# Source histogram, lane counts and running base of a graph network kernel: one product with 128 columns of weights in place of two with 64

## The chip, the core and the metric

The kernel runs on one core of one Trainium2 chip. The metric is the device time of one execution in microseconds (us); the figure compared is the median of several runs. TensorE's rows in the profile show two granted clocks, 0.50 (1.2 GHz) and 1.00 (2.4 GHz), and means between them where a stretch holds both.

## What is computed

Four graph layers on 12500 nodes with 64 features, 400000 edges sorted by destination, each layer with a normalisation ahead of it and a residual behind it:

```python
h = jnp.maximum(_layernorm(x), 0.0)
x = x + L0(h)   # edge network relu([x_i, x_j - x_i] @ W1 + b1) @ W2 + b2, then segment_max over dst
h = jnp.maximum(_layernorm(x), 0.0)
x = x + L1(h)   # sum over edges of x[src] * rsqrt(out_deg[src]), times rsqrt(in_deg), @ W + b, leaky relu
h = jnp.maximum(_layernorm(x), 0.0)
x = x + L2(h)   # two rounds of mean over incoming edges, each with a dense layer
h = jnp.maximum(_layernorm(x), 0.0)
x = x + L3(h)   # x @ W_self.T + b_self + segment_sum(x[src] * edge_weight, dst) @ W_neigh.T + b_neigh
```

`out_deg` is the number of edges that leave each node: a histogram of `src`. It is one of the things that the changed products compute.

## The kernel before

128 partitions ("lanes") hold 3125 consecutive edges each, and the edge loops walk them in 125 blocks of 25 columns (`K`), five blocks (`R`) to an iteration of a hardware loop. Each engine's program is written by hand; semaphores alone order them.

**Stage of layer 0 (`body0`).** For each block, GpSimd (POOL) gathers 25 columns of rows of `tab_edge_b` into a ring of five slots with one indirect DMA each (L632) and one more for the keys (L640). VectorE (DVE, `slot0`) adds, scans maxima column by column (L1393) and, between those, makes one-hot batches with one instruction each (`row_onehots`, L685): first the batches of the block's own `src` numbers (`hist_batch`: 16 columns, then 9; one-hots of the quotient, 128 wide, and of the remainder, 98 wide), then eight batches of 16 columns for `block_counts` (`count_batch`). TensorE (PE) runs in this order: two transposes of keys (L1939, L1940), the first batch of transposes of the ring (`turn`, L1929), `hist_counts(b, 0)` over 16 columns and `hist_counts(b, 1)` over 9, then in turn more transposes, the edge products (L1952) and `block_counts`. ScalarE (ACT) empties what PE makes: transposes at L1753, counts at L1737, 4 banks for each batch of 16 columns.

For each column c, `hist_counts` adds into PSUM `mixed` the product of the quotient's one-hots (weights) with the remainder's (moving, 98 columns), which is the histogram, and the product of an identity `ident_b` with the same remainder's one-hots, which counts by lane. Both go through a helper that makes each as two products with 64 columns of weights, the output's partitions 0 to 63 and 64 to 127:

```python
def halves(to, by_q, by_r, start, stop):
    for k in range(0, P, D):
        last = e.matmul(to[k:k + D, :], by_q[:, k:k + D], by_r, start=start, stop=stop, skip_group_check=True)
    return last
```

That is 4 products for a column, 100 for a block. The last product of each of the two calls raises `histed`; DVE's `count_batch(b, r, 0)` waits for the first (it overwrites the one-hots that the first 16 columns used) and `count_batch(b, r, 1)` for the second. `block_counts` uses `halves` as well, 256 products for a block, into the two banks `bk`.

**Stage of layer 3 (`body4`).** For each block DVE computes target rows for 25 columns of messages, and POOL scatters them with 25 indirect DMAs (L1180). PE's only work in the loop is the running base: when DVE has raised `looked`, 25 pairs of halves add `ident_b` times the block's one-hots `oh_lane` to PSUM `kp`, and the last raises `based`; DVE waits for it before it makes the next block's one-hots.

Between the two stages stand the dense sums of layers 1 to 3 (L769, L775, L728, L730), which the change does not touch. Ahead of `body0`, `count_tensor` (L479) makes products with 128 columns of weights and 98 moving columns, in groups of five; behind `body4`, `unit` (L2004) makes products with 128 columns of weights and 64 moving columns.

Of the kernel before, what the change touches and what calls it, by code (L numbers as in the profile page):

```python
# [19 lines left out]
K = 25  # L20
# [17 lines left out]
HIST = [range(0, VS), range(VS, K)]  # L38
# [19 lines left out]
def build(nc, x, src, dst, edge_weight, l0_w1, l0_b1, l0_w2, l0_b2, l1_w, l1_b,  # L58
# [7 lines left out]
    with ctx:  # L66
# [60 lines left out]
        ident_b = sb("ident_b", [P, P], bf16)  # L127
# [73 lines left out]
        hist, pa, pb = mixed[:, 0:TILES], mixed[:, TILES:TILES + P], mixed[:, TILES + P:TILES + 2 * P]  # L201
        cnt = mixed[:, TILES + 2 * P:2 * TILES + 2 * P]
        kp = ps("kp", [P, 512])
        base, iota_p = kp[:, 0:TILES], kp[:, P:2 * P]
# [10 lines left out]
        def mm_banks(name, u):  # L215
# [20 lines left out]
        ohq = [h_half[:, u * P * VS:(u + 1) * P * VS].rearrange("p (k q) -> p k q", q=P) for u in range(2)]  # L236
        ohr = [h_half[:, 2 * P * VS + u * TILES * VS:2 * P * VS + (u + 1) * TILES * VS]
               .rearrange("p (k q) -> p k q", q=TILES) for u in range(2)]
# [22 lines left out]
        oh_lane = m_half[:, 2 * K * TILES:3 * K * TILES].rearrange("p (k q) -> p k q", q=TILES)  # L261
# [39 lines left out]
        def gate(e):  # L301

            e.sem_inc(sem("gate_" + e.engine.name), 1)
# [1563 lines left out]
        def _(e):  # L1867
# [27 lines left out]
            def halves(to, by_q, by_r, start, stop):  # L1895

                for k in range(0, P, D):
                    last = e.matmul(to[k:k + D, :], by_q[:, k:k + D], by_r, start=start, stop=stop, skip_group_check=True)  # L1898
                return last

            def hist_counts(b, h):

                wait(e, "batched", b * (VB + 2) + (h + 1))
                gate(e)
                for c in range(len(HIST[h])):
                    first = isinstance(b, int) and b + h + c == 0
                    halves(hist, ohq[h][:, c, :], ohr[h][:, c, :], first, c == len(HIST[h]) - 1)
                    last = halves(cnt, ident_b, ohr[h][:, c, :], False, c == len(HIST[h]) - 1)
                last.then_inc(sem("histed"), 1)

            def block_counts(b, v):
# [75 lines left out]
            def body4(i):  # L1987
                for r in range(R):
                    wait(e, "looked", i * R + (r + 1))
                    gate(e)  # L1990
                    for j in range(K):
                        last = halves(base, ident_b, oh_lane[:, j, :], False, j == K - 1)
                    last.then_inc(sem("based"), 1)
            loop(e, body4)

# [36 lines left out]
```

## Time and profile before

| | |
|---|---|
| device time, median of 3 runs | 18454.92 us (18447.9 to 18476.08) |
| profiled execution: span from first to last instruction | 13809.8 us |
| what lies around the span (median less span) | 4645.1 us |
| PE busy, weight loads busy | 7082.0 us, 5084.7 us |
| DVE busy | 9045.7 us (66%) |
| ACT busy | 5948.2 us (43%) |
| POOL busy | 7815.4 us (57%) |
| stage `body0` | about 560 to 5280 us of the span |
| stage `body4` | about 9010 to 13100 us |

The profile gives the span of the profiled execution and no device time of its own for it, so its own time is taken as the median, with the 4645.1 us around the span. In the rows below a group of instructions is "engine line operation out<-in, weights, moving columns, type, xcount"; PE is a product, PEld a load of its weights, and "idle before <-releaser" is the time in which the engine stood still before it and what ended that. "issue" is idle time that no event in the profile explains.

### The profile page before, as it was taken

How to read it: one execution, taken by the hardware profiler on the slowest of the kernel's cores; microseconds unless marked ns; L12 is line 12 of the kernel's file. 1: busy time of each engine (PE TensorE's matmuls, PEld its weight loads, DVE VectorE, ACT ScalarE, POOL GpSimd, SP SyncE). 2: the span in 40 equal slices, each digit the busy share in tenths (PEclk: the TensorE clock that was granted, in tenths of full speed). 3: DMA queues.
4: the chain of work that ended last, by engine and by line, in shares of the span. 5: the costliest groups of instructions: out<-in, count | busy, mean ns of one | idle time of the engine just before them, and what ended most of it. 6: DMA issues, size and time to landing. Idle time of an engine off the chain costs nothing. (4 is left out here: it accounts for less than half of the span.)

```text
span 13809.8 us, 283975 instructions
## 1 busy us (share of the span) xinstructions
PE 7082.0 (51%) x96792; PEld 5084.7 (37%) x96792; DVE 9045.7 (66%) x17848; ACT 5948.2 (43%) x10705; POOL 7815.4 (57%) x7194
## 2 busy tenths in 40 slices
PE   2266666666666663998899999700000000000066
PEld 1155555555555552554455555400000000000055
DVE  5388888888888886444444344466666666666585
ACT  0144444444444443776777677522222222222201
POOL 5677777777777773111111111367777777777700
PEclk9866666666666666999899899755555555555598
DMA  7333333333333333886688588422222222222197
GB/s 308 144 112 113 112 114 114 119 112 112 113 112 115 115 114 94 261 265 220 200 263 267 172 265 263 160 72 66 63 66 66 66 63 66 63 63 66 60 361 241
DMA packets 1274431, 1981.83 MB, mean 144 GB/s; under 512 B 256937, under 2 KB 987918, under 8 KB 1268737
## 3 DMA queue, kind: packets, MB, share of 16 engines
q1 hardware_dynamic: 867553, 1059.78, 24.4%
q10 hardware_dynamic: 174288, 612.09, 12.0%
q0 software_dynamic: 231664, 297.80, 8.1%
q8 instruction: 558, 9.14, 0.3%
q14 instruction: 368, 3.01, 0.1%
HBM read 1167.21 MB, written 815.55 MB: 144 GB/s over the span
## 5 line engine op out<-in xcount | busy, mean ns | idle before, releaser
L632 POOL DMA_INDIRECT RF<-tab_edge_b,idx x3125 | 3541.2, 1133 | 1030.6 <-issue 948.6
L1180 POOL DMA_INDIRECT records<-RF,idx x3125 | 3130.6, 1002 | 984.5 <-issue 984.5
L1737 ACT ACTIVATE X<-bk 128x392 uint8<-128x392 f32 x4000 | 1782.6, 495 | 1565.0 <-PE bk L1898 1548.0
L685 DVE TENSOR_TENSOR HM<-iota_b,eqw 128x2048 bf16<-128x2048 bf16 x2000 | 2201.7, 1101 | 342.7 <-PE bk L1898 197.6
L1898 PE MATMUL bk<-HM 128*64 128x98 bf16 x32000 | 1583.2, 247 | 1306.7 <-ACT X L1737 672.8
L1898 PE MATMUL kp<-HM,ident_b 128*64 128x98 bf16 x6250 | 281.7, 283 | 3805.4 <-DVEq L1646 3805.4
L876 POOL DMA_INDIRECT agg<-RF,lastT x372 | 536.9, 1443 | 2856.9 <-ACT RF L808 2766.0
L769 PE MATMUL tp<-HM,RF 128*64 128x512 bf16 x12276 | 2001.2, 379 | 7.9 <-ACT HM L728 2.0
L1898 PEld LDWEIGHTS bk<-HM 128*64 128x64 bf16 x32000 | 1239.8, 134 | 1653.2 <-issue 1571.3
L1898 PEld LDWEIGHTS kp<-HM,ident_b 128*64 128x64 bf16 x6250 | 261.7, 168 | 3826.3 <-issue 3826.3
L775 PE MATMUL om<-HM,RF 128*64 128x512 bf16 x6138 | 1442.3, 379 | 0.0
L769 PE MATMUL tp<-RF 128*64 128x512 bf16 x5952 | 1032.7, 381 | 201.4 <-ACT RF L728 201.4
L769 PEld LDWEIGHTS tp<-HM,RF 128*64 128x64 bf16 x12276 | 854.2, 110 | 651.6 <-issue 52.3
L730 DVE CAST HM<-dst_f 128x4096 bf16<-128x4096 uint8 x186 | 426.8, 2294 | 739.1 <-DMA dst_f<-counts 390.1
L1828 ACT ACTIVATE RF<-qblk 128x50 f32<-128x50 f32 x125 | 31.7, 254 | 1978.9 <-DMA records<-RF,idx 1904.2
L1393 DVE SCALAR_TENSOR_TENSOR RF<-RF,dupjunk 128x64 f32<-128x64 f32 x3124 | 865.8, 277 | 27.3
L1393 DVE SCALAR_TENSOR_TENSOR RF<-RF,dupjunk,om 128x64 f32<-128x64 f32 x3124 | 841.2, 269 | 0.4
L728 ACT ACTIVATE RF<-dst_f 128x4096 bf16<-128x4096 uint8 x186 | 672.7, 3617 | 343.1 <-PE tp L769 342.0
L728 ACT ACTIVATE HM<-dst_f 128x4096 bf16<-128x4096 uint8 (+1 forms) x186 | 702.2, 3822 | 102.5 <-PE tp L769 102.5
L775 PE MATMUL om<-RF 128*64 128x512 bf16 x2976 | 722.6, 381 | 0.0
L728 ACT ACTIVATE HM<-crow 128x4096 bf16<-128x4096 uint8 x186 | 670.6, 3606 | 6.4 <-DMA crow<-counts 4.5
L1898 PE MATMUL mixed<-HM 128*64 128x98 bf16 x6250 | 498.6, 272 | 329.8 <-DVE HM L685 278.2
(362 smaller groups left out, 14805.4 us busy)
## 6 DMA issues: line engine op xcount, KB each, us to landing
dst_f<-counts SPq DMA_DIRECT2D x465, 512.0 KB, 4.6
RF<-first_rows SPq DMA_DIRECT2D x250, 800.0 KB
counts<-X ACTq DMA_DIRECT2D x250, 784.0 KB
records<-RF ACTq DMA_DIRECT2D x88, 1960.0 KB, 8.2
RF<-records SPq DMA_DIRECT2D x220, 784.0 KB
crow<-counts SPq DMA_DIRECT2D x279, 512.0 KB, 4.7
first_rows<-RF ACTq DMA_DIRECT2D x25, 4000.0 KB, 49.5
edge_rows<-RF ACTq DMA_DIRECT2D x125, 800.0 KB, 8.0
```

What stands on the lines that cost most here:

```text
L632: e.indirect_dma_start(out=ring[:, r, j, :], out_offset=None, in_=table[:, :], in_offset=bass.IndirectOffsetOnAxis(ap=idx[:, r, j:j + 1], ...
L685: return e.tensor_tensor(to[:, 0:n, :].rearrange("p k (q h) -> p k q h", h=2), iota_b[:, 0:m].rearrange("p (q h) -> p q h", h=2).unsqueeze ...
L728: e.activation(to, of, ACT.Copy).then_inc(sem("widened_A"), 1)
L730: e.tensor_copy(to, of).then_inc(sem("widened_D"), 1)
L769: last = e.matmul(tp[u][k * D:(k + 1) * D, :], hi_mid[:, t, k * D:(k + 1) * D], part, start=t == 0, stop=t == TILES - 1, skip_group_check= ...
L775: return e.matmul(om[u][k * D:(k + 1) * D, :], low[:, t, :], part, start=t < 2, stop=t >= TILES - 2, skip_group_check=True)
L876: e.indirect_dma_start(out=agg[:, :], out_offset=bass.IndirectOffsetOnAxis(ap=lastT[:, g * GB + k:g * GB + k + 1], axis=0), in_=out_rows[g ...
L1180: e.indirect_dma_start(out=records[:, :], out_offset=bass.IndirectOffsetOnAxis(ap=idx2[:, r, j:j + 1], axis=0), in_=msgs[MSG_OF[r]][:, j, ...
L1393: e.scalar_tensor_tensor(out=buf[:, r, j, :], in0=prev, scalar=mask[:, j:j + 1], in1=this, op0=op0, op1=op1).then_inc(sem(chain.name), 1)
L1737: e.activation(staged[u].rearrange("p (r k) -> p r k", k=P)[:, :, k:k + 4], bk[s % 2][:, 0:4 * TILES].rearrange("p (k r) -> p r k", k=4), ...
L1828: e.activation(msgs[MSG_OF[r]][:, :, RW - 2:RW], qblk[:, r, :].unsqueeze(2).broadcast_to([P, K, 2]), ACT.Copy)
L1898: last = e.matmul(to[k:k + D, :], by_q[:, k:k + D], by_r, start=start, stop=stop, skip_group_check=True)
```

## The change

`hist_counts` and the running base of `body4` use a new helper that makes one product with all 128 columns of weights where there were two of 64. `block_counts` keeps `halves`.

```diff
+            def whole(to, by_q, by_r, start, stop):
+
+                return e.matmul(to, by_q, by_r, start=start, stop=stop, skip_group_check=True)
+
             def hist_counts(b, h):
...
                 for c in range(len(HIST[h])):
                     first = isinstance(b, int) and b + h + c == 0
-                    halves(hist, ohq[h][:, c, :], ohr[h][:, c, :], first, c == len(HIST[h]) - 1)
-                    last = halves(cnt, ident_b, ohr[h][:, c, :], False, c == len(HIST[h]) - 1)
+                    whole(hist, ohq[h][:, c, :], ohr[h][:, c, :], first, c == len(HIST[h]) - 1)
+                    last = whole(cnt, ident_b[:, :], ohr[h][:, c, :], False, c == len(HIST[h]) - 1)
                 last.then_inc(sem("histed"), 1)
...
                     for j in range(K):
-                        last = halves(base, ident_b, oh_lane[:, j, :], False, j == K - 1)
+                        last = whole(base, ident_b[:, :], oh_lane[:, j, :], False, j == K - 1)
                     last.then_inc(sem("based"), 1)
```

On PE, at the start of a block's `hist_counts` (`mixed` is the PSUM tile, `HM` holds the one-hots), the program before has, with the output's rows and columns behind the names:

```order
L1929 MATMUL tp<-ident,RF 128x128 x4
L1898 MATMUL mixed<-HM 64x98 x2
L1898 MATMUL mixed<-HM,ident_b 64x98 x2
L1898 MATMUL mixed<-HM 64x98 x2
L1898 MATMUL mixed<-HM,ident_b 64x98 x2
```

and the changed one, whose lines lie four further down and whose `whole` is L1903:

```order
L1933 MATMUL tp<-ident,RF 128x128 x4
L1903 MATMUL mixed<-HM 128x98
L1903 MATMUL mixed<-HM,ident_b 128x98
L1903 MATMUL mixed<-HM 128x98
L1903 MATMUL mixed<-HM,ident_b 128x98
```

Each x2 has become one product; the pattern goes on for 25 columns. Nothing else stands in another place on PE, and the programs of DVE, ACT and SP are the same.

## Rows read from the trace of the kernel before

**Rows 1.** The page: the span, and each engine's busy time and instructions.
```profile
span 13809.8 us, 283975 instructions
PE 7082.0 (51%) x96792; PEld 5084.7 (37%) x96792; DVE 9045.7 (66%) x17848; ACT 5948.2 (43%) x10705; POOL 7815.4 (57%) x7194
```
**Rows 2.** Busy time by window, one in each stage; then PEclk, DMA share, GB/s.
```profile
3000.00:3500.00 500.00, 310.43 (x5227) 261.84 (x5222) 435.05 (x1003) 220.10 (x489) 386.57 (x346) 0.68 0.36 112
10000.00:11000.00 1000.00, 67.60 (x1500) 62.81 (x1500) 638.12 (x1288) 288.43 (x1064) 766.88 (x766) 0.50 0.21 65
```
**Rows 3.** Waits from 1000 to 5000 us, in `body0`: us in total, times, longest.
```profile
POOL RF L632 <- issue: 806.6, 2647, 0.3
...
DVE lane_keys L1435 <- issue: 99.2, 21, 5.5
...
DVE HM L685 <- PE mixed L1898: 74.4, 94, 3.9
...
POOL RF L632 <- DMA cix<-chunk_lin: 34.9, 10, 5.5
POOL crow L640 <- issue: 32.3, 106, 0.3
```
**Rows 4.** List by line, whole span: busy us, mean ns, idle before, three releasers.
```profile
L632 POOL DMA_INDIRECT RF<-tab_edge_b,idx x3125 | 3541.2, 1133 | 1030.6 <-issue 948.6 <-DMA cix<-chunk_lin 52.7 <-DMA tab_edge_b<-HM 29.2
...
L685 DVE TENSOR_TENSOR HM<-iota_b,eqw 128x2048 bf16<-128x2048 bf16 x2000 | 2201.7, 1101 | 342.7 <-PE bk L1898 197.6 <-PE mixed L1898 101.5 <-PE om L1952 33.9
```
**Rows 5.** Timeline of PE in one block: start us, us; the 50 pairs of `hist_counts`.
```profile
3059.99 0.29 PE L1898 MATMUL mixed<-HM 128*64 128x98 bf16 x2 [2.22 <-DVE HM L685]
...
3060.21 0.32 PE L1898 MATMUL mixed<-HM,ident_b 128*64 128x98 bf16 x2
...
3063.96 0.27 PE L1898 MATMUL mixed<-HM,ident_b 128*64 128x98 bf16 x2
3064.16 0.66 PE L1929 MATMUL tp<-ident,RF 128*128 128x128 f32 x4
```
**Rows 6.** Timeline of DVE in the same block, at `count_batch(b, r, 0)`.
```profile
3062.96 1.22 DVE L685 TENSOR_TENSOR HM<-iota_b,eqw 128x2048 bf16<-128x2048 bf16 x1 [0.37 <-PE mixed L1898]
```
**Rows 7.** Timeline of PE, first block of an iteration: a pause inside `hist_counts`.
```profile
1138.28 0.32 PE L1898 MATMUL mixed<-HM,ident_b 128*64 128x98 bf16 x2
1140.50 0.29 PE L1898 MATMUL mixed<-HM 128*64 128x98 bf16 x2 [1.91 <-issue]
```
**Rows 8.** Timeline of DVE in that block.
```profile
1143.15 1.22 DVE L685 TENSOR_TENSOR HM<-iota_b,eqw 128x2048 bf16<-128x2048 bf16 x1 [2.49 <-PE mixed L1898]
```
**Rows 9.** Timeline of PE: products that have 128 columns of bf16 weights already.
```profile
42.19 0.59 PE L479 MATMUL mixed<-HM 128*128 128x98 bf16 x5 [0.99 <-DVE HM L465]
...
272.16 1.67 PE L1884 MATMUL mixed<-eqw,hT 128*128 128x128 bf16 x14 [2.19 <-DVE eqw L676]
...
13110.58 5.28 PE L2004 MATMUL bk<-RF 128*128 128x64 bf16 x96 [90.00 <-DVE RF L685]
```
**Rows 10.** Durations by line: ns min/median/max, first and last start; weights, moving columns.
```profile
L479 PE MATMUL mixed<-HM x125: 260/282/285, 40.6 to 79.0; 128*128 128x98 bf16 x125
...
L1898 PE MATMUL mixed<-HM x6250: 203/282/291, 569.4 to 5244.3; 128*64 128x98 bf16 x196
```
**Rows 11.** Busy time by window: around the last row of rows 9, and around rows 5.
```profile
13110.00:13116.00 6.00, 5.28 (x96) 5.18 (x97) 3.87 (x8) 0.70 (x3) 0.00 (x0) 0.50 0.99 319
...
3059.00:3064.00 5.00, 4.01 (x100) 4.04 (x100) 4.52 (x10) 1.09 (x2) 3.78 (x5) 0.50 1.01 407
```
**Rows 12.** Timeline of PE: one bank of `block_counts` at either granted clock.
```profile
3055.34 0.95 PE L1898 MATMUL bk<-HM 128*64 128x98 bf16 x16 [0.36 <-ACT X L1737]
...
3065.97 0.55 PE L1898 MATMUL bk<-HM 128*64 128x98 bf16 x16 [0.26 <-issue]
```
**Rows 13.** Timeline in `body4`: PE's running base, and DVE's next use of `kp`.
```profile
9107.92 2.25 PE L1898 MATMUL kp<-HM,ident_b 128*64 128x98 bf16 x50 [21.51 <-DVEq L1646]
...
9129.69 2.71 DVE L1645 TENSOR_TENSOR HM<-HM,kp 128x2450 f32<-128x2450 bf16 x1
```

## The prediction

> **What bounds the kernel now.** The two stages that the change touches have different limits, so I read the page's totals first and then each stage by itself. The page gives a span of 13809.8 us, with DVE and POOL the busiest engines in the sum [rows 1]. The window in `body0` shows PE busy 310 of 500 us, DVE 435, POOL 387; the window in `body4` shows PE busy 68 of 1000 us and POOL 767 [rows 2].
>
> In `body4` the 766 scatters of the window leave 1000 - 766.88 = 233 us, 0.304 us for each. That is the pause that POOL makes between any two of its indirect DMAs in `body0` as well ("issue", 806.6 / 2647 = 0.305 us) [rows 2, 3]. So POOL never waits for anybody there: it is the limit.
>
> In `body0` two engines run almost level. POOL has 386.57 us of work and 346 pauses of 0.305 us in 500 us, 492 in all. Its only waits for others are 34.9 us out of 4000, and 52.7 us in the whole span (the releaser DMA `cix<-chunk_lin`, index loads that SP sends when DVE has finished a scan) [rows 2 to 4]. DVE is the engine that these waits come from, and it never waits for the gathers. So DVE, with its own waits, sets the pace, and POOL stands right behind it. What DVE waits for is what the change can move: over the span its batches wait 197.6 us for `block_counts`, 101.5 us for `hist_counts` (`mixed`) and 33.9 us for the edge products (`om`) [rows 4]. The window from 1000 to 5000 us holds 106 blocks (one key gather each), 37.7 us for a block, and 94 of them have a wait for `mixed`, 74.4 us in all [rows 3].
>
> These waits are of two kinds. In an ordinary block DVE waits 0.37 us for the end of the first 32 pairs [rows 6]. In the first block of an iteration PE pauses after its eighth product with "issue" as the cause, here 1.91 us, and DVE then waits 2.49 us [rows 7, 8]. Such starts are the 21 in the window at which DVE itself stops for 99.2 us in total [rows 3]. With 0.37 us for 94 - 21 = 73 ordinary waits (27 us), 47 us are left for the 21 starts, 2.3 us each, which fits the row.
>
> **The pace of the products.** It carries everything else. Before, 50 pairs start between 3059.99 and 3063.96 us: 3.97 / 49 = 0.081 us for a pair, at a granted clock of 0.50, which is the lower level, 1.2 GHz [rows 5, 11]. 98 columns at 1.2 GHz take 98 / 1.2 = 82 ns, so a pair costs what one product costs: the two halves already run side by side, and halving the number of products saves no array time. What one whole product costs is shown by `count_tensor`, whose products have the very shape (128 columns of bf16 weights, 98 moving columns): five take 0.59 us, the last of them some 0.28, so (0.59 - 0.28) / 4 = 0.078 us for each [rows 9, 10]. Their median duration, 282 ns, is that of the halves as well [rows 10]. The bounds for the new step are 0.078 and, from the row with 128 moving columns, (1.67 - 0.31) / 13 = 0.105 us, where 0.31 is an estimate for the last product (282 ns and 30 more columns) [rows 9]. I take 0.081, nearest to the row with the same shape: cost 0.
>
> Could wide weights show behind a product? `unit` has 128 columns of bf16 weights and 64 moving ones: 96 products in 5.28 us, (5.28 - 0.24) / 95 = 0.053 us at granted clock 0.50 (0.24 is my estimate for the last one) [rows 9, 11]. So such a load fits into 0.053 us, well under the 0.081 of 98 columns. The Trainium skill, "TensorE: Matmul & The Clock Gate", section "LDWEIGHTS (loading the stationary operand)", says otherwise: a load costs its columns divided by 1.2 in ns, an estimate of 107 ns for 128, and by it the sum would be that of rival B. The same page's part on Fast Weight Load excepts loads of exactly 128 columns that aren't fp32, and the trace agrees with the exception. Whoever leaves these sentences out still has 0.053.
>
> **The change part by part, in `body0`.**
>
> 1. The last half. A pair's row lasts 0.32 us and a product 0.282 [rows 5, 10], so the second half starts 0.04 us behind the first, and the semaphore hangs on the second. A whole product ends with the first. In the ordinary blocks DVE's wait of 0.37 us ends 0.04 earlier: 73 x 125 / 106 = 86 blocks, 3 us.
> 2. The pause at an iteration's start. It comes after 8 products, which is after a fixed number of instructions [rows 7]. With whole products the 8 done before it are worth 16 halves, so 24 products remain of the first 32, where 28 pairs did: 4 x 0.081 = 0.32 us less of DVE's 2.3 us, at 24 starts: 8 us. The bounds are 0 (it sits elsewhere now) and its whole length, about 2 x 24 = 48 us.
> 3. From halves to transposes. The last pair starts at 3063.96 and the next transpose at 3064.16, 0.20 us against a step of 0.08 [rows 5]. If the surplus of 0.12 is the price of going from 64-column products to 128-column ones, it leaves this place. It makes the edge products earlier, for which DVE waits 33.9 us in all [rows 4]. Bounds 0 and 0.12 x 125 = 15 us; I take 6, since under half of the blocks have that wait at all. The Trainium skill, "TensorEngine Tiling (Array Packing)", section "Key Properties", says that changing the tiling mode drains TensorE; by it this term is wholly real, by the pause alone it may be something else.
> 4. `block_counts`, all DVE, ACT, POOL and SP instructions and every wait are as before: 0.
>
> **In `body4`** PE ends the base at 9107.92 + 2.25 = 9110.2 us and DVE reads `kp` at 9129.69 [rows 13]; 19 us cover a burst of 2.3. Were it half or double, nobody would notice. 0 us. If this cover went, the loop would still be POOL's.
>
> The sum is 3 + 8 + 6 = 17 us less. Late next is POOL: what DVE gains beyond POOL's 52.7 us of waits [rows 4] would be spent waiting for gathers. Against 18454.92 us (the span and 4645.1 us around it, taken as unchanged; I use the median because the profiled execution has no time of its own) that gives **18438 us**. Seventeen us are 0.1%; about 0.2%, 37 us, is what a measurement of this kernel can tell from no change.
>
> **The rivals.**
>
> - **A, the pause goes.** Half as many products and loads to bring in could let PE start an iteration without its pause, and the early blocks too. DVE would gain up to 48 us from term 2, and 9 from the others, 57, cut to POOL's 52.7: about 18402 us. For it speaks that the pause has "issue" as its cause; against it that DVE stops at the same place for 4.7 us each with a program that does not change [rows 3].
> - **B, wide weights show (slower).** Place: the first 32 products of each `hist_counts`, whose end DVE awaits. If a load of 128 columns cannot hide, a product costs 0.105 us, the upper bound above, against 0.081 for a pair: 0.024 x 32 = 0.77 us for a block, all of it on DVE, x 125 = 96 us, 18551 us. It decides from a step of about 0.091 on (0.3 us for a block, 37 us). For it speaks the width; against it both rows of 128-column weights at the lower clock.
> - **C, the clock (slower).** In this stage the clock is at its higher level part of the time, mean 0.68 [rows 2]. If PE with half as many instructions were granted it less often, one more bank group for each block would run as the 0.95 us row and not as the 0.55 us row [rows 12]. DVE's batches hide part of it; I take 0.3 us for a block, 37 us: 18492 us. Against it: the array streams the same columns for the same time.
> - **D, nothing at all**, or the change does not act as it reads (both halves still issued): 18455 us. The printed program speaks against the second.
>
> **How the numbers follow.** The forecast has 0.58, A 0.13, B 0.07, C 0.09, D 0.13. Forecast and D lie within 0.2%: 0.71, and half of C, just at the border, makes it 0.76. Faster by over 0.2% is A, 0.13. Slower is B and the rest of C, 0.11. The range reaches from A (18402, rounded to 18400) to C (18492, rounded to 18490); left out are B and what lies beyond A and C, under 2 in 10.
>
> **What the changed profile would show.** 6250 products on `mixed` in 128*128 form and 3125 on `kp`, 50 of the former starting within 4.0 us of each other. If a step is 0.10 or more, B holds. DVE's wait for `mixed` should fall from 101.5 to about 90 us, and in an ordinary block from 0.37 to 0.33; if to 50 or less and POOL's waits vanish, A. The pause stands after eight products, four columns in. Transposes should follow the last product by about 0.08 us. The mean clock in the window from 3000 to 3500 us should stay near 0.68; below 0.6, C. `body4` should be as long as before. What would make me wrong is a change in POOL's mean of 1133 ns, or in the time around the span, for neither of which I have a row that links it to PE.

## The result and the profile after

| | before | changed |
|---|---|---|
| device time, median of 4 runs each | 18465.02 us (18447.9 to 18476.08) | 17591.63 us (17580.4 to 17620.77) |
| ratio, 95% interval | | 0.9527 (0.9513 to 0.954) |
| profiled execution | span 13809.8 us [rows 1] | span 17619.0 us, own time 17620.77 us |

The changed kernel is 4.7% faster, 873 us; the prediction said 17 us. The table also holds a contradiction: the changed kernel is faster, and its span is 3809 us longer than the one shown of before. The page of the changed kernel (the span, and busy time by engine) answers to [rows 1]:

```profile
span 17619.0 us, 265225 instructions
PE 7501.6 (43%) x87417; PEld 5424.8 (31%) x87417; DVE 9024.0 (51%) x17848; ACT 5983.1 (34%) x10705; POOL 7386.3 (42%) x7194
```

9375 products and their loads are gone, as the diff says. The work of each engine is within 7% of that of [rows 1]; what has grown is the time without work. Busy time by window, one window in each stage, shows it against [rows 2]: in `body0` DVE works 268 us of 500 where it worked 435, PE gets 2829 products done where it did 5227 (50 of them for each block have gone with the change), POOL 209 DMAs where it did 346.

```profile
3000.00:3500.00 500.00, 215.78 (x2829) 178.44 (x2830) 268.32 (x619) 137.29 (x304) 210.84 (x209) 0.60 0.23 70
...
14000.00:15000.00 1000.00, 55.03 (x625) 50.32 (x625) 530.09 (x1082) 243.40 (x878) 626.30 (x635) 0.50 0.18 54
```

The list by line over the whole span answers to [rows 4]. POOL waited 52.7 us for `cix<-chunk_lin`, that is, for DVE; now it is 3269.5. DVE's batches waited 342.7 us in all, now 3182.6, most of it for "remote". That word stands for a signal (a semaphore's update) near whose time the trace has no instruction that could have sent it.

```profile
L632 POOL DMA_INDIRECT RF<-tab_edge_b,idx x3125 | 3180.6, 1018 | 4271.4 <-DMA cix<-chunk_lin 3269.5 <-issue 915.5 <-DMA tab_edge_b<-HM 86.4
...
L685 DVE TENSOR_TENSOR HM<-iota_b,eqw 128x2048 bf16<-128x2048 bf16 x2000 | 2189.8, 1095 | 3182.6 <-remote 1832.4 <-PE bk L1898 1119.8 <-PE mixed L1903 154.0
```

So the profile shown of before and the profile after are not the same kind of execution, and their difference is not the change. The first thing to run was the kernel before, unchanged.

### The profile page after: what moved, and what is told of

It is laid out like the page before. It is cut to its first block and busy times, and to the rows that moved or that the text cites. A ratio compares the mean times of both kernels' runs of the same rounds, so it can differ in the third digit from the quotient of the medians.

```text
span 17619.0 us, 265225 instructions
## 1 busy us (share of the span) xinstructions
PE 7501.6 (43%) x87417; PEld 5424.8 (31%) x87417; DVE 9024.0 (51%) x17848; ACT 5983.1 (34%) x10705; POOL 7386.3 (42%) x7194
## 5 line engine op out<-in xcount | busy, mean ns | idle before, releaser
L632 POOL DMA_INDIRECT RF<-tab_edge_b,idx x3125 | 3180.6, 1018 | 4271.4 <-DMA cix<-chunk_lin 3269.5
L1180 POOL DMA_INDIRECT records<-RF,idx x3125 | 3085.5, 987 | 1863.7 <-issue 995.0
L685 DVE TENSOR_TENSOR HM<-iota_b,eqw 128x2048 bf16<-128x2048 bf16 x2000 | 2189.8, 1095 | 3182.6 <-remote 1832.4
L1898 PE MATMUL bk<-HM 128*64 128x98 bf16 x32000 | 1754.1, 257 | 3379.6 <-issue 1604.4
L1898 PEld LDWEIGHTS bk<-HM 128*64 128x64 bf16 x32000 | 1336.6, 141 | 3822.4 <-issue 3750.0
L1903 PE MATMUL kp<-HM,ident_b 128*128 128x98 bf16 x3125 | 275.2, 282 | 4647.5 <-DVEq L1646 3024.9
L1903 PEld LDWEIGHTS kp<-HM,ident_b 128*128 128x128 bf16 x3125 | 251.6, 142 | 4671.9 <-issue 4671.9
L775 PE MATMUL om<-HM,RF 128*64 128x512 bf16 x6138 | 1326.3, 379 | 0.0
L1753 ACT ACTIVATE hT<-tp 128x512 f32<-128x512 f32 x500 | 255.7, 511 | 2112.3 <-remote 1962.8
L1628 DVE SCALAR_TENSOR_TENSOR tp<-tp,mblk,RF 128x64 f32<-128x64 f32 x1875 | 548.3, 292 | 652.7 <-DVE tp L1628 361.8
L1956 PE MATMUL om<-w_diag,hT 128*128 128x128 f32 (+1 forms) x3250 | 718.1, 371 | 190.5 <-issue 188.2
L1956 PEld LDWEIGHTS om<-w_diag,hT 128*128 128x128 f32 (+1 forms) x3250 | 642.6, 280 | 233.2 <-issue 220.1
```

What stands on the lines that cost most here:

```text
L632: e.indirect_dma_start(out=ring[:, r, j, :], out_offset=None, in_=table[:, :], in_offset=bass.IndirectOffsetOnAxis(ap=idx[:, r, j:j + 1], ...
L685: return e.tensor_tensor(to[:, 0:n, :].rearrange("p k (q h) -> p k q h", h=2), iota_b[:, 0:m].rearrange("p (q h) -> p q h", h=2).unsqueeze ...
L775: return e.matmul(om[u][k * D:(k + 1) * D, :], low[:, t, :], part, start=t < 2, stop=t >= TILES - 2, skip_group_check=True)
L1180: e.indirect_dma_start(out=records[:, :], out_offset=bass.IndirectOffsetOnAxis(ap=idx2[:, r, j:j + 1], axis=0), in_=msgs[MSG_OF[r]][:, j, ...
L1628: loop_chain(e.scalar_tensor_tensor(out=in_bank(j), in0=prev, scalar=mblk[:, 0, j:j + 1], in1=fill[:, r, j, :], op0=ALU.mult, op1=ALU.add))
L1956: last = e.matmul(om[q % 2][:, k * P:k * P + m], hT[0:m, q % 2, k * P:(k + 1) * P], w_diag[0:m, 0:m], start=True, stop=True)
```

## The experiments

The runs were made in seven groups. Those of one group share a chip and the runs of before on it, so every ratio is against before on the same chip. In the diffs - and + stand against the changed kernel, or against the one before where that is said. The stages are measured throughout by one view: the first and last start of POOL's key gathers (L640, `body0`) and of its scatters (L1180, `body4`).

**1. Before, and each half of the change alone** (one chip; before 18499.95 us). `e1_before` has no edit. `e2_hist_only` keeps `halves` in `body4`, `e3_base_only` in `hist_counts`. `e4_all_whole` uses `whole` in `block_counts` too:

```diff
-                        last = halves(bk[s % 2][:, m * TILES:(m + 1) * TILES], ohq[v % 2][:, s * 4 + m, :],
-                                      ohr[v % 2][:, s * 4 + m, :], True, True)
+                        last = whole(bk[s % 2][:, m * TILES:(m + 1) * TILES], ohq[v % 2][:, s * 4 + m, :],
+                                     ohr[v % 2][:, s * 4 + m, :], True, True)
```

> The kernel before, unchanged, to see in a profile of its own the execution that takes 18460 us. Theory S (TensorE is starved of instructions in the timed executions; the profile shown of before, span 13809.8 us, caught an execution in which it was not): time 18460 us, and if the profile is of a timed kind its span is about 18460 us, with pauses of 0.7 us or a multiple between TensorE's products in body0 and waits with 'issue' in body4. Rival F (the form: pairs of halves cost more array time than whole products): the span may be either, but products within a burst stand 0.082 us a pair, with no pauses of that kind. Rival R (the 4645 us around the span are work outside the profiled span that the change shortened): span again 13810 us with a time of 18460 us.

> Whole products in the histogram and lane counts only; the running base keeps its halves. The change took out 9375 products and 874 us, 0.093 us for each. Theory S: 6250 products fewer, 6250 x 0.093 = 583 us, about 17880 us. Rival F, where only products on the path to a wait count: all of the gain, about 17590 us, since in body4 TensorE's burst is covered by 19 us. A gain of the first block only: under 100 us, 18370 us.

> Whole products in the running base of layer 3 only; the histogram keeps its halves. Theory S: 3125 products fewer at 0.093 us, 290 us, about 18170 us. Rival F: nothing, 18460 us, since this burst has cover. The two single changes should add up to the whole change's 874 us under S.

> Whole products everywhere, in block_counts too: 16000 products fewer than the change. Theory S: 16000 x 0.093 = 1490 us less than 17592, about 16100 us, unless the starving ends before that; its floor is the span of the profile shown of before, 13810 us. Rival F with the step of the rows before (0.081 us for either form): no change against 17592 us. A rival in which the gain came from having fewer changes between 64-column and 128-column products: at most the same order as the change itself, 874 us, for 2 changes of form a block removed there and some 8 here: 874/250 x 1000 = 3500 us, 14100 us.

Measured: 18502.53 us, ratio 1.0004 (0.9995 to 1.0014); 17828.86, 0.9652 (0.9623 to 0.9681); 18235.14, 0.9849 (0.9829 to 0.9869); 17460.82, 0.9427 (0.9384 to 0.9471). The page of `e1_before`:

```profile
span 18475.6 us, 283975 instructions
PE 8047.2 (44%) x96792; PEld 5624.9 (30%) x96792; DVE 9018.5 (49%) x17848; ACT 5970.2 (32%) x10705; POOL 7266.0 (39%) x7194
```

The same program has a span of 18475.6 us here and of 13809.8 in [rows 1]; its profiled execution took 18477.39 us, so less than 2 us lie around the span. The 4645.1 us "around the span" are therefore time inside it: the profile shown of before and the times shown come from two kinds of execution. They are called the short kind (13.8 ms) and the long kind (18.5 ms) here.

The two halves add up: -671 us and -265 us make -936, and the change gives between -873 and -968 in the groups of the long kind. The source histogram and lane counts are about 70% of it, the running base about 30%.

Where the time goes is visible in one block of `e1_before`. PE's timeline, at `hist_counts` and what follows it, answers to [rows 5]:

```profile
4702.80 0.29 PE L1898 MATMUL mixed<-HM 128*64 128x98 bf16 x2 [2.21 <-DVE HM L685]
...
4705.17 0.29 PE L1898 MATMUL mixed<-HM,ident_b 128*64 128x98 bf16 x2
4705.80 0.31 PE L1898 MATMUL mixed<-HM 128*64 128x98 bf16 x2 [0.33 <-issue]
...
4706.61 0.30 PE L1898 MATMUL mixed<-HM,ident_b 128*64 128x98 bf16 x2
...
4722.20 0.24 PE L1898 MATMUL mixed<-HM,ident_b 128*64 128x98 bf16 x1 [1.18 <-issue]
...
4728.51 0.47 PE L1929 MATMUL tp<-ident,RF 128*128 128x128 f32 x1 [1.04 <-issue]
...
4737.15 0.86 PE L1898 MATMUL bk<-HM 128*64 128x98 bf16 x16
```

The first 28 pairs start within 2.4 us, at the pace of [rows 5]. Then PE stands still again and again, with "issue" as the cause, and starts anew 0.7 or 1.4 us (once 2.1) after the start before. Four products come in such a step at first and one at the end; the 22 pairs that are left take some 18 us. Transposes and edge products then come one every 1.4 us, with one step of 2.1. After about 4736 us everything runs at full pace again, a bank of 16 halves in 0.86 us. POOL's timeline over the same time has the other half of the picture:

```profile
4699.23 0.94 POOL L632 DMA_INDIRECT RF<-tab_edge_b,idx  x1 [31.01 <-DMA cix<-chunk_lin]
...
4731.85 0.95 POOL L640 DMA_INDIRECT crow<-kr,cix  x1 [0.30 <-issue]
...
4763.67 0.95 POOL L632 DMA_INDIRECT RF<-tab_edge_b,idx  x1 [30.87 <-DMA cix<-chunk_lin]
```

Its 26 indirect DMAs of a block fill 33 us. PE's crawl in these rows begins 6 us after the first of them (at 4705.2) and ends 3.4 us after the last (at 4736.2). Then POOL waits 31 us, because DVE, held up, has not finished the scans that free the ring. DVE's timeline shows how long it waits at `count_batch(b, r, 0)` and `(b, r, 1)`, where it needs the first and the second `histed`, and at the second the first edge products as well. The first answers to [rows 6], 12.70 us where 0.37 stood:

```profile
4718.09 1.23 DVE L685 TENSOR_TENSOR HM<-iota_b,eqw 128x2048 bf16<-128x2048 bf16 x1 [12.70 <-remote]
...
4737.56 1.23 DVE L685 TENSOR_TENSOR HM<-iota_b,eqw 128x2048 bf16<-128x2048 bf16 x1 [16.32 <-PE om L1952]
```

The first wait shows something that PE's timeline hides. The product that raises the first `histed` is in the row at 4706.61, which ends at 4706.91, and DVE starts 11.2 us after that, when the signal comes ("remote"). In the short kind the two lie 0.15 us apart (in `e17_after_fourth` the same product starts at 3052.92 and lasts 0.28 us, and DVE starts at 3053.35, below). So in the long kind the end of a row of PE is not the time at which the engine that waits for it can go on.

The changed kernel in the same place, PE's timeline:

```profile
5136.87 0.24 PE L1903 MATMUL mixed<-HM 128*128 128x98 bf16 x1 [2.79 <-DVE HM L685]
...
5139.36 0.28 PE L1903 MATMUL mixed<-HM,ident_b 128*128 128x98 bf16 x1
...
5141.16 0.20 PE L1903 MATMUL mixed<-HM 128*128 128x98 bf16 x1 [0.22 <-issue]
...
5146.13 1.10 PE L1956 MATMUL om<-w_diag,hT 128*128 128x128 f32 x4 [1.03 <-issue]
5151.44 0.38 PE L1898 MATMUL bk<-HM 128*64 128x98 bf16 x4 [4.21 <-DVE HM L685]
...
5167.95 0.24 PE L1898 MATMUL bk<-HM 128*64 128x98 bf16 x1 [1.16 <-issue]
...
5170.70 0.93 PE L1898 MATMUL bk<-HM 128*64 128x98 bf16 x16 [1.11 <-ACT X L1737]
```

and DVE's:

```profile
5148.42 1.22 DVE L685 TENSOR_TENSOR HM<-iota_b,eqw 128x2048 bf16<-128x2048 bf16 x1 [8.96 <-remote]
...
5169.84 1.23 DVE L685 TENSOR_TENSOR HM<-iota_b,eqw 128x2048 bf16<-128x2048 bf16 x1 [18.28 <-remote]
```

Fifty products stand where a hundred stood, so in PE's rows the burst is nearly over when the crawl begins: all of it takes 4.5 us, not 20, and the crawl then meets the first bank of `block_counts`. The means over the blocks of these rows are 28.5 us for the burst in `e1_before` and 5.3 in the changed kernel, 23 us less; but a block takes only 5 us less (next table). DVE's rows say why. The row of the product with the first `histed` ends at 5139.64, and DVE goes on at 5148.42; the rows of the first edge products end at 5147.23, and DVE goes on at 5169.84. Counted from the first product, DVE's two waits end after 11.6 and 33.0 us here, where they end after 15.3 and 34.8 us in the block of `e1_before`: these two blocks differ by 3.7 and 1.8 us where DVE waits, and not by 16.

This gives the theory W: while POOL issues indirect DMAs, the other engines get instructions slowly (a product is two, its load and itself); the time is lost by instructions in that stretch and not by columns. The rows just read leave a second reading of its first half, in which PE is given its instructions and is late in finishing them or in telling of it. By either the loss in the stretch goes by the number of instructions; which of them holds was not tested. The table has the first and last start of each stage's POOL work, and its length.

| run | key gathers L640 | us | scatters L1180 | us |
|---|---|---|---|---|
| before, the profile shown | 546.7 to 5173.1 | 4626 | 9020.3 to 13101.9 | 4082 |
| `e1_before` | 599.6 to 8630.7 | 8031 | 12549.3 to 17705.9 | 5157 |
| changed | 602.0 to 8026.8 | 7425 | 11942.2 to 16856.7 | 4914 |
| `e2_hist_only` | 602.4 to 7985.2 | 7383 | 11898.5 to 17055.6 | 5157 |
| `e3_base_only` | 600.0 to 8673.1 | 8073 | 12583.4 to 17489.6 | 4906 |
| `e4_all_whole` | 601.6 to 7942.9 | 7341 | 11841.3 to 16726.7 | 4885 |

Between `e1_before` and the changed kernel lie 606 us in `body0` and 243 in `body4`, 849 of the 857 us between the two spans. These two profiles are of different groups; two more of the changed kernel, in experiments 4 and 5, have 7635 and 7614 us for `body0`. On one chip, from `e1_before` to `e2_hist_only`, it is 648 us, 5.2 us for each block. Each part acts on its own stage, and the other stage stays within 42 us. Between `e1_before` and the profile shown lie 3405 and 1075 us, 4480 of 4666: the long execution is longer in just the two stages in which POOL issues indirect DMAs all the time.

`e4_all_whole` saves 42 us of `body0` against `e2_hist_only`, though it takes 128 instead of 256 products from each block; its expectation was far off. Most of `block_counts` lies behind the crawl, where one product more or less costs next to nothing. In the crawl its banks wait for ACT's copies, and ACT waits for PE's signal. PE's timeline at one bank, four whole products, and ACT's at the copies before and behind it:

```profile
4389.91 0.48 PE L1903 MATMUL bk<-HM 128*128 128x98 bf16 x4 [9.93 <-issue]
```

```profile
4389.27 0.50 ACT L1737 ACTIVATE X<-bk 128x392 uint8<-128x392 f32 x1 [6.46 <-remote]
4394.88 0.50 ACT L1737 ACTIVATE X<-bk 128x392 uint8<-128x392 f32 x1 [5.11 <-remote]
```

ACT's first copy ends at 4389.77, and PE's four products start 0.14 us later, so the 9.93 us named "issue" are in truth a wait for that copy. Their rows end at 4390.39, all four at full pace, and the copy that waits for them starts at 4394.88, 4.5 us later. Here no product is late by its row, and its signal is.

**2. Is it the number of instructions, and is it POOL?** (another group; before 18609.17 us)

`e5_count_back` keeps the wide products and gives the count back: a product of one moving column, with the same weights, into an unused column of the bank.

```diff
+                e.matmul(spare_column, by_q, by_r[:, 0:1], start=False, stop=stop, skip_group_check=True)
                 return e.matmul(to, by_q, by_r, start=start, stop=stop, skip_group_check=True)
```

`e6_quarters`, against the kernel before, makes four products of 32 columns in `hist_counts`:

```diff
+                for k in range(0, P, 32):
+                    last = e.matmul(to[k:k + 32, :], by_q[:, k:k + 32], by_r, start=start, stop=stop, skip_group_check=True)
```

`e7_half_gathers` takes 12 of 25 gathers from each block, with the waits adjusted to it:

```diff
-            for j in range(K):
+            for j in range(0, K, 1 if isinstance(i, int) else 2):
```

`e8_double_stores` stores each block's counts a second time:

```diff
+                    e.dma_start(counts_twice[h][bass.ds(b, 1), :, :, :].rearrange("b q r k -> q (b r k)"),
+                                staged[u][:, h * RH * P:(h + 1) * RH * P]).then_inc(sem(f"counts_out{u}"), 16)
```

> The changed kernel with a one-column product, same weights, ahead of each whole product, into a PSUM column that nobody reads: the number of TensorE's products and loads is again that of the kernel before, while the whole form stays. Theory W (in each block, while POOL issues its gathers, the other engines get their instructions slowly, some 0.7 us a step, so the number of instructions counts and not the array's work): back to about 18500 us. Rival F (what counted was the form or the array time of the halves): stays at about 17590 us, since a one-column product takes hardly any array time.

> The kernel before with four products of 32 columns in place of each two halves in the histogram and lane counts: 100 products more in each block, 12500 in all. A plain price for a product (671 us for the 6250 that the histogram alone took out, 0.107 us each): 1340 us more, 19840 us. Theory W with its bound: the slow stretch of a block lasts only as long as POOL's 26 gathers, 34 us; a block with no progress at all in it would take 34 + 36.5 = 70.5 us against the 65.5 us of the kernel before, so at most 5 us x 125 = 625 us more, 19120 us. Rival F (array time alone, quarters side by side): 18500 us.

> The changed kernel leaves out 12 of 25 gathers of each block from the second iteration on (the maxima of layer 0 are then of stale rows); POOL's 14 instructions take 18 us and not 34. Theory W: of the 60.5 us of a block 34 are slow ones, in which about 11 us of the 37.7 us of work get done (60.5 - 34 = 26.5 are left for the rest). With 18 slow us, 6 us of work get done in them and 31.7 follow: 50 us a block, 10.5 x 120 = 1260 us less, about 16330 us. Rival Q (the stores of counts and edge rows at the block's start hold up the instruction supply): no change but the traffic of the gathers, within 100 us of 17590 us.

> The changed kernel stores each block's counts twice (a second copy to a tensor of its own), 1.6 MB more a block, some 4 us of traffic at 390 GB/s. Rival Q: if the stores cause the slow stretch, it gets much longer, up to twice, 1000 us or more above 17590 us. Theory W: at most the traffic itself where ACT waits for it, under 4 us x 125 = 500 us, more likely under 100 us, and the slow stretches end with POOL's last gather as before.

Measured: `e5_count_back` 18623.94 us, ratio 1.0006 (0.9997 to 1.0016); `e6_quarters` 18802.59, 1.0106 (1.0089 to 1.0123); `e7_half_gathers` 15852.71, 0.8521 (0.8504 to 0.8539); `e8_double_stores` 17696.59, 0.9502 (0.9483 to 0.9521).

`e5_count_back` is the sharpest of them. The wide products are all there and the whole gain is gone: it is the number of PE's products and loads, not their form, width or columns. Its waits from 1000 to 6000 us (us in all, times, longest) name the place:

```profile
PE mixed L1903 <- issue: 922.4, 774, 3.3
PE mixed L1904 <- issue: 911.8, 771, 2.7
```

In a run of the changed kernel (`e12_after_again`) the same view has one such line, and it is a twelfth of their sum:

```profile
PE mixed L1903 <- issue: 148.7, 134, 3.2
```

`e6_quarters` adds 12500 products and 12500 loads, and 193 us come of them, 1.5 us for a block. At 1.4 us for a product that would be far more. Doubled once more, most of the burst falls behind the stretch: by PE's rows its mean goes from 32.6 us in `e5_count_back`, with 100 products, to 34.3 with 200. A stretch of 33 us bounds what can be lost in it.

`e7_half_gathers` shortens the stretch itself; POOL's timeline has it at 17 us instead of 33:

```profile
3022.80 0.94 POOL L632 DMA_INDIRECT RF<-tab_edge_b,idx  x1 [32.12 <-DMA cix<-chunk_lin]
...
3039.15 0.94 POOL L640 DMA_INDIRECT crow<-kr,cix  x1 [0.30 <-issue]
```

POOL is not what `body0` waits for here (it stands still for 32 us of each block), and yet the stage falls to 5842 us, where the changed kernel has 7425 above and 7614 and 7635 in the two repeats below. Some 1580 to 1790 us for 125 blocks are 13 to 14 us for a block, near the 16 by which the stretch is shorter. The order of size was expected, the full amount was not. This shows that the slow stretch goes with POOL's indirect DMAs; whether it is their issue or their transfers was not separated. The stores are not the cause: with twice as many, the ratio is within those of the changed kernel itself, below.

**3. Counts alone, and fewer instructions ahead of ACT and PE** (a third chip). `e9_counts_only` has `whole` in `block_counts` alone. `e10_no_gates` is `e4_all_whole` without the carrier instruction (`gate`) between a wait and ACT's copy; `e11_fewer` takes away as well PE's in `block_counts`, `hist_counts` and `body4`:

```diff
                     wait(e, "banked", b * CW + (v * 4 + s + 1))
-                    gate(e)
...
                 wait(e, "batched", b * (VB + 2) + (h + 1))
-                gate(e)
...
                     wait(e, "bank_out", b * CW + (v * 4 + s - 1))
-                    gate(e)
...
                     wait(e, "looked", i * R + (r + 1))
-                    gate(e)
```

> Whole products in block_counts only; histogram, lane counts and running base keep their halves: 16000 products fewer than before. Price for each product as in the change (0.093 us): 1490 us less, a ratio of 0.92 to the kernel before. Theory W: in the kernel before the slow stretch is over when the histogram's products are (its burst of 100 products lasts 28.5 us in the profile), and block_counts runs behind it at full pace, so what is taken out there is outside: a ratio within 0.995 and 1.00.

> Whole products everywhere (as in e4_all_whole, ratio 0.943) and, on ACT, one instruction less ahead of each of the 32 copies of a block: the semaphore increment that carried the wait is gone, the copy waits itself. At full pace this is worth nothing (17 ns each, ACT is idle half the time). Theory W, if ACT too is short of instructions in the slow stretch (one copy with its two other instructions takes 5.6 to 6.5 us there, about 1.9 us each): a third less for each of the 4 to 6 copies in the stretch, up to 8 us a block, a ratio down to 0.90. If only TensorE is short of instructions and ACT waits for it: 0.943.

> As e10_no_gates, and the same carriers left out on TensorE ahead of each bank of block_counts, ahead of the two calls of hist_counts and ahead of the running base. Theory W: a little less again than e10_no_gates, 0.005 to 0.02 of ratio. A rival by which only matmuls and weight loads count: the same as e10_no_gates.

Measured: 13825.91 us, ratio 0.9999 (0.9988 to 1.001); 13809.37, 0.9988 (0.9978 to 0.9997); 13747.42, 0.9938 (0.9919 to 0.9958). The expectations were written for the long kind and could not be judged: **before took 13829.54 us on this chip** (13788.19 to 13858.89, 19 runs). That is the short kind, the one of the profile shown, now with times beside it. There all three edits do nothing or little; the largest step is that from `e10_no_gates` to `e11_fewer`, PE's carriers, 0.9988 to 0.9938.

**4. The same in the long kind** (before 18638.13 us), with the change beside it.

> The change itself once more. On a chip where the kernel before takes about 13830 us (no slow stretches): the prediction's sum, 17 us less, a ratio of 0.9988, and at most 53 us less, 0.996. On a chip where it takes about 18500 us: 0.9527 as before. If the change were worth its 870 us everywhere, the ratio on the fast chip would be 0.937.

> Whole products in block_counts only. On a chip with slow stretches: theory W 0.995 to 1.00, a price for each product 0.92. On a chip without: 1.000 as in e9_counts_only.

> Whole products everywhere and no carriers of waits on ACT's copies and on TensorE. On a chip with slow stretches: theory W, down to 0.89, and under 0.943 in any case if ACT's instructions count there. On a chip without: 0.994 as in e11_fewer.

> Whole products everywhere and no carriers on ACT's copies. On a chip with slow stretches: between e14 and 0.943, 0.90 if ACT's instructions count as TensorE's do. On a chip without: 0.999 as in e10_no_gates.

Measured: the change 17681.1 us, ratio 0.9484 (0.9471 to 0.9497); counts alone 18626.43, 0.9992 (0.9983 to 1.0001); `e11_fewer` again 17462.45, 0.9361 (0.9347 to 0.9375); `e10_no_gates` again 17543.56, 0.9411 (0.9397 to 0.9426).

Counts alone take away 16000 products, more than the change's 9375, and move nothing. That is W's most telling case: in the kernel before they start where the crawl has ended. The burst ahead of them still crawls, as its waits from 1000 to 6000 us say (1522.3 us for the same line in `e1_before`):

```profile
PE mixed L1898 <- issue: 1807.1, 1592, 3.3
```

Together with whole histograms, which bring the first banks into the stretch, they give 0.0073 more here (0.9484 to 0.9411). How much of that is ACT's missing carriers can be said only across groups (`e4_all_whole` had 0.9427, `e15_no_gates_again` 0.9411, with overlapping intervals): hardly anything, so that expectation fell. PE's missing carriers give another 0.005. They gave the same 0.005 in the short kind, so this step says nothing for W. `e11_fewer` is the best version in both kinds: 0.9361 and 0.9938.

**5. The change in either kind.** `e16_after_third` (before 18588.45 us), and `e17_after_fourth` with `e18_all_whole_again`, whose group turned out to be of the short kind (before 13845.93 us, 13820.4 to 13868.42, 21 runs).

> The change itself. On a chip where the kernel before takes about 13830 us: the prediction's sum, 17 us less, a ratio of 0.9988, at most 53 us less, 0.996. On a chip where it takes about 18500 us: 0.95 once more.

> The change itself. On a chip where the kernel before takes about 13830 us: the prediction's sum, 17 us less, a ratio of 0.9988, at most 53 us less, 0.996. On a chip where it takes about 18500 us: 0.948 to 0.953 once more.

> Whole products everywhere, on the same chip as e17. On a chip with slow stretches: 0.005 to 0.01 of ratio below e17, since with whole products TensorE takes part of block_counts inside the stretch and 128 products less a block lie mostly behind it. On a chip without: the same as e17 within 0.001.

Measured: the change in the long kind once more 17620.82 us, ratio 0.9481 (0.9468 to 0.9494). In the short kind it took 13854.85 us, **ratio 1.0007 (0.9998 to 1.0016)**, and everything whole 13837.7, 0.9996 (0.9987 to 1.0005), no different within the intervals. The page of `e17_after_fourth`, against [rows 1]:

```profile
span 13833.1 us, 265225 instructions
PE 7084.3 (51%) x87417; PEld 5097.9 (37%) x87417; DVE 9048.7 (65%) x17848; ACT 5943.4 (43%) x10705; POOL 7812.7 (56%) x7194
```

Its window in `body0`, against [rows 2]:

```profile
3000.00:3500.00 500.00, 309.76 (x4549) 262.94 (x4549) 432.82 (x996) 218.47 (x485) 387.31 (x344) 0.67 0.37 114
```

Of the profiles of the changed kernel only this one may be laid beside the profile shown of before. `body0` takes 4624 us there (4626 before), `body4` 4081 (4082).

## Why the prediction was wrong, point by point

**The step that failed** is "Against 18454.92 us (the span and 4645.1 us around it, taken as unchanged)". `e1_before` shows that under 2 us lie around the span. The 4645 us were lost inside `body0` and `body4`, and the change takes 849 us of them. The prediction closed with the time around the span as something that would make it wrong, and gave it no chance and no price. The Trainium skill, "Runtime: NRT & Kernel Launch", section "The ~15µs preamble/postamble breakdown", puts the difference between the profile's total and the reported time at about 6 us for any kernel, the total being the larger. Here the time exceeds the span from first to last instruction, by under 2 us in `e1_before` and `e17_after_fourth` alike, and 4645.1 is far from either figure.

**What bounds the kernel.** "DVE sets the pace, and POOL stands right behind it" holds in the short kind alone. In the long kind POOL waits half of a block for DVE, and DVE for signals of PE that come late. The waits of the changed kernel from 1000 to 7000 us answer to [rows 3]; part of PE's "issue" in them may be a wait for ACT, as at the bank of `e4_all_whole` above:

```profile
POOL RF L632 <- DMA cix<-chunk_lin: 2634.6, 98, 34.1
...
DVE HM L685 <- remote: 1485.2, 154, 26.2
...
PE bk L1898 <- issue: 1322.3, 439, 15.6
...
DVE HM L685 <- PE bk L1898: 919.5, 316, 19.0
```

**The pace of the products: right.** A whole product costs what a pair cost. PE's timeline in one block of `e17_after_fourth`, against [rows 5]:

```profile
3050.43 0.24 PE L1903 MATMUL mixed<-HM 128*128 128x98 bf16 x1 [2.24 <-DVE HM L685]
...
3054.39 0.28 PE L1903 MATMUL mixed<-HM,ident_b 128*128 128x98 bf16 x1
3054.47 1.08 PE L1933 MATMUL tp<-ident,RF 128*128 128x128 f32 x4
```

DVE's timeline in the same block, against [rows 6]:

```profile
3053.35 1.22 DVE L685 TENSOR_TENSOR HM<-iota_b,eqw 128x2048 bf16<-128x2048 bf16 x1 [0.33 <-PE mixed L1903]
```

(3054.39 - 3050.43) / 49 = 0.081 us. Rival B, with its decision at 0.091, is refuted, by rows of the changed kernel itself. The rule in the Trainium skill, "TensorE: Matmul & The Clock Gate", section "LDWEIGHTS (loading the stationary operand)", that spoke for B (an estimate of 107 ns for a load of 128 columns) does not set the pace here: the step is 0.081 us, and the page's exception for such loads, which the prediction names, is borne out.

**Term 1, right:** DVE's ordinary wait is 0.33 us, from 0.37.

**Term 2, wrong.** The pause at an iteration's start comes after two products now, not after eight, and is not shorter. PE's timeline in `e17_after_fourth`, against [rows 7]:

```profile
3010.73 0.28 PE L1903 MATMUL mixed<-HM,ident_b 128*128 128x98 bf16 x1
3014.21 0.24 PE L1903 MATMUL mixed<-HM 128*128 128x98 bf16 x1 [3.21 <-issue]
```

"After a fixed number of instructions" failed. Why the pause lies there is not shown: in `e9_counts_only`, whose program is shorter too but keeps the halves in `hist_counts`, it still comes after eight products. The list by line, against [rows 4], has DVE's wait for `mixed` at 98.2 us (101.5 before), where about 90 was forecast:

```profile
L685 DVE TENSOR_TENSOR HM<-iota_b,eqw 128x2048 bf16<-128x2048 bf16 x2000 | 2203.6, 1102 | 332.3 <-PE bk L1898 196.4 <-PE mixed L1903 98.2 <-PE om L1956 23.3
```

The 8 us of this term did not come, and rival A, which needed the pause to go, is refuted.

**Term 3, right in its mechanism.** The transpose starts 0.08 us behind the last product, not 0.20, and DVE's wait for `om` falls from 33.9 to 23.3 us. The Trainium skill, "TensorEngine Tiling (Array Packing)", section "Key Properties", says that a change of the tiling mode drains TensorE. The trace agrees: the 0.12 us are gone where the mode no longer changes. The time did not follow: POOL waits 52.8 us for DVE as before, its mean for a gather is 1134 ns (1133 before), and the 15 us less of DVE's three waits (333.0 to 317.9) are lost in the spread of single executions.

**Clock.** The window from 3000 to 3500 us has a mean of 0.67 (0.68 before) in `e17_after_fourth`: rival C is refuted. **D** describes the short kind best: 17 us of 13845.93 would be 0.9988, outside the interval from 0.9998 to 1.0016.

**`body4`: wrong in the long kind.** "19 us cover a burst of 2.3" and "if this cover went, the loop would still be POOL's" both failed there. The waits of `e1_before` from 13000 to 17000 us show PE's 50 halves held up, and DVE waiting:

```profile
DVE HM L685 <- remote: 942.0, 49, 23.9
...
PE kp L1898 <- issue: 675.6, 343, 22.2
```

With the base whole (`e3_base_only`) the same window has 178.1 us for the first of them:

```profile
DVE HM L685 <- remote: 178.1, 29, 17.5
```

The mean burst, by PE's rows, falls from 9.9 to 2.2 us. POOL is no longer the limit there: before its scatters it waits 1154.1 us for DVE (DVEq), and in the profile shown of before all its 3125 waits there are "issue", 984.5 us. `e1_before`, the releasers of L1180:

```profile
  DVEq L325: 1154.1, 61
  issue: 968.0, 3064
```

**What is not settled.** What decides the kind. Of seven groups five were of the long kind and two of the short, each the same in all its runs; the profile shown of before is of the short kind, and the times that stand with it are of the long one. That it belongs to the chip is not shown either: experiments 2 (long) and `e17_after_fourth` (short) are recorded with one chip number, and whether they are one chip is not known. It could not be chosen. By what path POOL's indirect DMAs slow PE is not shown, nor whether its instructions come late or its work is finished or signalled late: the rows with "issue" in `e1_before` speak for the first, the bank in `e4_all_whole` for the second. `e5_count_back`, counts alone and `e7_half_gathers` fit both. It is hardly the size or speed of the instruction blocks that are fetched. The DMA view from 1000 to 5000 us (queue, packets, MB, share of 16 engines) has in `e1_before`

```profile
q8 instruction: 236, 3.87, 0.4%
```

and in the profile shown of before 424 such packets at 0.7%: 0.4% and 0.7% of 16 engines x 4000 us are 256 and 448 us, about 1.1 us a packet in both, as far as the rounding carries. The Trainium skill, "Runtime: NRT & Kernel Launch", section "Instruction fetch mechanics", says that instructions come in blocks of 16 KiB and that crossing into the next is mostly hidden; the size agrees (3.87 MB / 236 = 16.4 KB), and no run here shows whether these blocks are what is late.

## What to carry to other kernels

Before any row is read, lay the profile's span beside the median of the timed runs: where they differ by more than a few us, the rows are of another kind of execution, and the missing time lies inside stages. Where an engine's timeline shows "issue" between small instructions while GpSimd issues indirect DMAs, count instructions in that stretch and not columns or busy time; merge small products there, and leave those outside alone. Price such an edit by when the engine that waits goes on, and not by the rows of the one that works: here the rows of the burst became 23 us shorter and the block 5.

## What the runs showed of the hardware that was not expected

- One program, unchanged, took 13829.54 and 13845.93 us in two groups of runs and 18465.02 to 18638.13 us in five others, steady within 0.6% in each.
- In the block shown of the long kind PE's rows have 28 pairs at 0.081 us each and then 22 pairs in some 18 us, in steps of 0.7 us and multiples, while POOL issues indirect DMAs; full pace returns 3.4 us after POOL's last. In the short kind the same products beside the same gathers lose nothing.
- In the long kind an engine that waits for PE goes on long after the row of PE's product has ended: 11.2 us in `e1_before`, 8.8 and 22.6 us in the changed kernel, 4.5 us in `e4_all_whole`, in the rows shown; in the short kind 0.15 us.
- DVE is slow in `body4` too. Its timeline in `e1_before` has steps of 0.29 us, each only 1.40 us after the one before:

```profile
15061.03 0.29 DVE L1628 SCALAR_TENSOR_TENSOR om<-om,mblk,RF 128x64 f32<-128x64 f32 x1 [1.11 <-DVE om L1628]
15062.43 0.29 DVE L1628 SCALAR_TENSOR_TENSOR om<-om,mblk,RF 128x64 f32<-128x64 f32 x1 [1.11 <-DVE om L1628]
```

- POOL's gathers are no slower in the long kind: a mean of 984 ns in `e1_before`, against 1133 in [rows 4].
